# Three rounded products for the second feed-forward product, and a new sharing of the rounding among ScalarE, VectorE and GpSimd

## The chip, the cores and the metric

One Trainium2 chip, one of its cores. The metric is the device time of one execution in microseconds. The kernel before takes 1093.89 us, the median of three runs (1093.78 to 1093.91).

## The reference

Four transformer blocks run one after the other on x of (4, 512, 256) in float32, steered by a conditioning vector of 256 for each of the four sequences. Called layer 0 to layer 3 here:

```
layer 0: h = film(rmsnorm(x)); one head of 256: softmax(q k^T / 16) v; x += out @ wp + b
         h = film(rmsnorm(x)); x += gelu(h @ w1 + b1) @ w2 + b2
layer 1: layernorm, scale and shift; 16 heads of 16, q and k normalised (cosine attention);
         x += gamma1 * (out @ wp + b);  x += gamma2 * (gelu(h @ w1 + b1) @ w2 + b2)
layer 2: layernorm, scale and shift; 16 heads, softmax(q k^T / 4) v; both branches gated as in layer 1
layer 3: 16 heads, softmax(q k^T) / 16; x += out @ wp + b; out = sln(x) + x, no feed-forward part
```

The feed-forward part goes from 256 to 1024 and back to 256, with the exact gelu. Layers 0, 1 and 2 have one.

## The kernel before, in words

Work is cut into 16 jobs, one for each layer and sequence (job j has layer j // 4 and sequence j % 4), each of 512 tokens, that is 4 token tiles of 128 partitions. X stays on the chip, tokens on the partitions.

**One list sets the order.** `PLAN` is a list of steps (kind, job or unit, index), built once from tables of due times (SINGLE0 to SINGLE3, FFN0 to FFN2, QKV, ATTN, FFN, FFN3 and so on, in ticks; a multi-head job has 16 ticks, a job of layer 0 is laid out on the same scale) and of patterns for the pairs of score products (PAIR and its like). Every engine walks through this same list and emits its own part of each step, so the list is the order on every queue: TensorE, ScalarE, VectorE, GpSimd, and SP, which issues all transfers. All waits are on semaphores that count the steps done. In layers 1 to 3 the score products of one job run beside the projections and the feed-forward part of the job before it.

**Precision.** Most products are made of three: an operand is split into a high part, rounded to float32r (`_h`), and a low part, the difference (`_l`), and `product` (L634 to L636) issues high x high, high x low and low x high. A few products use plain float32: the transposes, the weighted sums over V (L751, L790), and the second feed-forward product (L831). A plain float32 matmul appears in the trace as two records.

**A job's feed-forward part.** norm2 gives tok2 (L1155, L1159), TensorE transposes it (hT2, L680), ScalarE scales and shifts it to `postT_f` (L882), VectorE rounds it to `postT_h` (L1059; ScalarE itself in layer 3), and GpSimd subtracts (L1388). fc1 makes 8 banks of 128x512, each by two triples. VectorE adds the bias on the way from the bank to `gT` (L1337). When all is there, the step gelu has ScalarE work in place on `gT`, two tiles of 512 at a time (L996). fc2 multiplies tiles of `gT`, 128 tokens as the stationary operand, with `w2_s` (256 columns moving), 8 products for each of 4 token tiles, one bank each. VectorE adds the bias row (L1344), GpSimd multiplies by the gate where there is one and adds to X (L1421, L1428).

**Layer 0's softmax.** VectorE takes the negated maximum of a bank (L1286) and scales it by 1/16 (L1287). ScalarE exponentiates with that bias and a scale of 1/16 and sums the row (L954). VectorE takes the reciprocal (L1292) and scales the row (L1293). Then the row is transposed (pT0) and multiplied with V. W_v and W_p are merged beforehand, so that this product is already the projection (L790), and VectorE adds it to X (L1312).

**The other layers' softmax.** VectorE reduces a first set of score products (max, L711 on TensorE and L1273 on VectorE), and the shift is folded into the second (scores, L736); ScalarE exponentiates (L944, L941); the weighted sums carry a column of ones for the denominator.

**Banks.** Seven banks of the matmul memory go round as a ring among all kinds of products (`RINGED`); the eighth collects the weighted sums. TensorE claims a bank when the reader of its last content is done.

**Weights.** w_qkv, w_p and w_1 are loaded in pieces of 256 KB. The first eight have places of their own (in `gT` and `probs`), later ones take turns in one buffer, `raw`: SP loads a piece when the one before is split, ScalarE rounds it (L854) and GpSimd subtracts (L1379). w_2 is loaded straight to `w2_s`.

**The rest that the change touches.** q and k: ScalarE writes the rounded part with the bias (L929), VectorE the low part from the same bank (L1243); likewise for the transposed attention output oT2 (L989, L1131). norm1 is on VectorE in layer 0 and on GpSimd (L1408) otherwise; norm2 is on VectorE.

Of the kernel before, what the change touches and what calls it, by code (L numbers as in the profile page):

```python
# [30 lines left out]
SCALE = (DIM ** -0.5, 1.0, HD ** -0.5, 1.0)  # L31
# [33 lines left out]
SINGLE0 = {"stat1": (-35.66,), "norm1": (95.09,), "hT1": (95.15, -51.96), "q": (52.71, 32.6), "k": (44.4, 51.22),  # L65
# [7 lines left out]
SINGLE2 = {"stat1": (-76.02,), "norm1": (-65.07,), "hT1": (-54.95, -50.83), "q": (-42.45, -39.93),
           "k": (-42.44, -37.11), "v": (-46.48, -29.71), "scores0": (-33.39, -32.62, -32.29, -30.97),
           "soft0": (-19.93, -18.73, -8.94, -3.07), "pT0": (-18.64, -15.94, 3.54, 6.39), "proj": (-1.74, 7.24),
           "stat2": (9.09,), "norm2": (11.69,), "bias": (-26.4,)}
FFN0 = {"hT2": (-6.48, -1.66), "fc1": (0.65, 1.43, 2.87, 7.57, 8.57, 10.48, 12.64, 13.3), "gelu": (10.5,),
        "fc2": (17.26, 18.61, 23.07, 32.19)}
FFN2 = {"hT2": (13.21, 13.55), "fc1": (23.3, 23.54, 23.67, 23.99, 25.74, 25.98, 26.03, 27.98), "gelu": (26.69,),
        "fc2": (31.27, 31.92, 33.07, 33.9)}  # L80
FIRST = {("merge", 0, 0): -124.29, ("mergerow", 0, 0): -109.34, ("v", 0, 0): -70.09, ("v", 0, 1): -67.94,
         ("modrow", 0, 1): -98.09, ("headscale", 1, 0): -51.0, ("mod", 0, 1): -57.81, ("split_wp", 0, 0): -182.81,
         ("split_w1", 0, 0): -41.76, ("split_w1", 0, 1): -31.99, ("split_w1", 0, 2): -9.65, ("split_w1", 0, 3): 5.96,
         ("load_w2", 0, 1): -31.88, ("load_w2", 0, 2): -21.35, ("load_w2", 0, 3): -16.6}
NEXT1 = {("modrow", 1, 0): -56.06, ("mod", 1, 0): -41.97, ("load_mod", 1, 1): -52.72, ("modrow", 1, 1): 27.9,
         ("mod", 1, 1): 31.64, ("load_gate", 1, 0): 12.82, ("split_qkv", 1, 0): 26.63, ("load_qkv", 1, 1): 7.49,
         ("split_qkv", 1, 1): 35.43, ("load_qkv", 1, 2): 10.53, ("split_qkv", 1, 2): 46.77,
         ("load_qkv", 1, 0): -34.16, ("vones", 4, 0): 44.63, ("vones", 5, 0): 66.11}
LEAD_IN = {"stat1": (-29.34,), "norm1": (-25.36,), "hT1": (-22.98, -21.7), "qktok": (-18.2, -17.08, -16.9, -16.15),
           "qkss": (-16.92, -16.51, -15.44, -14.66), "qkroot": (-12.97,), "v": (-13.86, -12.83),  # L90
           "qknorm": (-12.92, -12.45, -12.35, -11.47), "q": (-10.22, -9.46), "k": (-9.65, -9.35),
           "stack": (-42.54, -35.32, -7.52, 4.91),
           "gmax": (-8.33, -7.93, -7.8, -6.86, -6.81, -5.35, -5.01, -4.95, -4.89, -4.54, -4.51, -3.48, -3.26, -2.88, -2.52, -2.18),
           "shift1": (-0.73, -0.59), "crow": (-40.19, -34.41, -22.72, 2.06)}
# [5 lines left out]
QKV = {"hT1": (-19.99, -13.91), "q": (-12.79, -9.58), "k": (-11.71, -11.59), "v": (-7.18, -6.37),  # L100
       "stack": (-8.14, -7.62, 1.2, 1.31), "stat1": (-28.09,), "norm1": (-26.73,)}
ATTN = {"oT1": (18.35, 18.35, 18.55, 18.63), "oT2": (19.0, 19.2), "proj": (20.28, 20.87), "stat2": (22.39,),
        "norm2": (24.27,)}
FFN = {"hT2": (25.31, 25.33), "fc1": (27.44, 27.6, 27.96, 28.05, 29.82, 30.13, 30.33, 30.64), "gelu": (30.28,),
# [215 lines left out]
def cond_blocks_kernel(nc, x, cond, cols, rows, wqkv, wp, w1, w2, wmod, wgate, out):  # L320
# [3 lines left out]
    with ExitStack() as ctx:  # L324
# [173 lines left out]
        def by_vector(a):  # L498

            return layer(a) < LAYERS - 1  # L500
# [1045 lines left out]
```

## Time and profile before

| | |
|---|---|
| median of three runs | 1093.89 us |
| the profiled execution | 1094.24 us, its span 1092.5 us |
| TensorE busy | 1062.0 us (97% of the span) |
| VectorE busy | 805.8 us (74%) |
| ScalarE busy | 659.8 us (60%) |
| GpSimd busy | 360.1 us (33%) |
| granted TensorE clock | full in nearly all of the span |

A matmul's record lasts from its start to its modelled end, and the next one starts before that end. So TensorE's busy share says whether it is fed, and the pace of a kind of matmul is read from start to start. In a row of groups stand the line of the kernel, the engine, the operation, what is written and read, the shape, the count, the busy time, the mean of one in ns, and the idle time of the engine just before these instructions with what ended it. The table's lines repeat on the page; the rows further down are those that the argument uses.

### The profile page before, as it was taken

What the parts mean: (1) busy time and instruction counts of PE and PEld (TensorE: products, weight loads), DVE (VectorE), ACT (ScalarE), POOL (GpSimd) and SP (SyncE); (2) the same over time, 40 slices, a digit from 0 to 9 for tenths busy, and PEclk for the clock granted to TensorE, in tenths of its full rate; (3) what the DMA queues carried; (4) which work ended last, traced back from release to release, by engine and by line L of the source; (5) the groups of instructions that cost most, each with busy time, mean ns of one, the idle gap of its engine ahead of it and who ended that gap; (6) DMA issues with size and microseconds to landing.
All of it is one profiled execution on the core that took longest, in us unless ns stands there. A gap on an engine that the chain in (4) does not pass through costs nothing.

```text
span 1092.5 us, 18693 instructions
## 1 busy us (share of the span) xinstructions
PE 1062.0 (97%) x6321; PEld 683.9 (63%) x6321; DVE 805.8 (74%) x1657; ACT 659.8 (60%) x1098; POOL 360.1 (33%) x339
## 2 busy tenths in 40 slices
PE   7999999999999999999999999999999999999995
PEld 5788788755755756657566556566566566645442
DVE  8676658686495584475986986976977967998984
ACT  3453342487467477565675774675765665686764
POOL 3333252422251433611521522422512513441523
PEclk9999999999999999999999999999999999999999
DMA  7100001213313222122122232212202203233301
GB/s 248 59 1 1 10 30 29 60 49 86 89 38 100 73 69 66 37 65 59 43 76 64 55 81 69 60 39 69 67 14 58 59 1 84 59 79 68 89 6 44
DMA packets 36381, 64.39 MB, mean 59 GB/s; under 512 B 7208, under 2 KB 22312, under 8 KB 36288
## 3 DMA queue, kind: packets, MB, share of 16 engines
q1 hardware_dynamic: 36288, 63.20, 21.9%
q8 instruction: 53, 0.87, 0.3%
q14 instruction: 40, 0.33, 0.1%
HBM read 22.90 MB, written 2.12 MB: 23 GB/s over the span
## 4 chain that ended last, share of the span: by engine, by line
PE 84%; DVE 10%; issue 2%; POOL 1%; ACT 1%; DMA 1%; SPq 0%; POOLq 0%; DVEq 0%; ACTq 0%
PE rings L831 15%; PE rings L751 14%; PE rings L736 12%; PE rings L634 10%; PE rings L636 9%; PE rings L635 9%; PE rings L711 4%; PE rings L790 2%; PE rings L680 2%; DVE m L1273 2%; PE rings L795 1%; PE rings L719 1%; PE rings L807 1%; DVE stats L1102 1%; PE rings L661 1%
## 5 line engine op out<-in xcount | busy, mean ns | idle before, releaser
L944 ACT ACTIVATE probs<-rings 128x512 f32<-128x512 f32 x566 | 299.5, 606 | 164.1 <-PE rings L711 96.3
L1273 DVE TENSOR_REDUCE m<-rings 128x1 fp32r<-128x512 f32 x512 | 318.8, 683 | 17.0 <-PE rings L711 14.2
L736 PE MATMUL rings<-SQ,SK 64*128 64x512 f32 x768 | 225.5, 436 | 3.7 <-ACT probs L941 1.1
L736 PEld LDWEIGHTS rings<-SQ,SK 64*128 64x128 f32 x768 | 106.7, 185 | 151.2 <-issue 76.6
L751 PE MATMUL rings<-probs,V 128*32 128x512 f32 x1536 | 198.6, 605 | 1.4 <-issue 1.4
L711 PE MATMUL rings<-SK,SQ 63*128 63x512 f32 x512 | 180.0, 442 | 0.8
L831 PE MATMUL rings<-w_s,gT 128*128 128x256 f32 x768 | 175.3, 382 | 0.3 <-DVE tmp L1344 0.3
L831 PEld LDWEIGHTS rings<-w_s,gT 128*128 128x128 f32 x768 | 142.5, 190 | 25.9 <-DVE gT L1337 3.4
L941 ACT ACTIVATE probs<-rings 128x1024 f32<-128x1024 f32 x101 | 98.2, 1031 | 39.8 <-PE rings L736 20.3
L1337 DVE TENSOR_SCALAR gT<-rings,colv 128x512 f32<-128x512 f32 x96 | 71.1, 748 | 39.7 <-PE rings L636 39.1
L1421 POOL TENSOR_TENSOR tmp<-tmp,gates 128x512 f32<-128x512 f32 x32 | 41.1, 1284 | 169.4 <-DVE tmp L1344 160.1
L711 PEld LDWEIGHTS rings<-SK,SQ 63*128 63x128 f32 x512 | 82.1, 185 | 12.3 <-ACT probs L944 8.9
L1388 POOL TENSOR_TENSOR hT_l<-hT_f,hT_h 128x512 fp32r<-128x512 f32 x30 | 38.7, 1291 | 150.2 <-DVE hT_h L1059 103.5
L1344 DVE TENSOR_TENSOR tmp<-rings,rowp 128x256 f32<-128x256 f32 x48 | 20.3, 424 | 89.3 <-PE rings L831 89.0
L751 PEld LDWEIGHTS rings<-probs,V 128*32 128x32 f32 x1536 | 35.8, 109 | 77.4 <-issue 66.5
L634 PE MATMUL rings<-postT_h,w_h 128*128 128x512 f32 x192 | 79.5, 414 | 0.5 <-POOL postT_l L1388 0.4
L636 PE MATMUL rings<-postT_h,w_l 128*128 128x512 f32 x192 | 75.4, 393 | 0.0
L635 PE MATMUL rings<-postT_l,w_h 128*128 128x512 f32 x192 | 75.3, 392 | 0.0
L1408 POOL TENSOR_SCALAR tok<-X,mv,rstd 128x256 f32<-128x256 f32 x48 | 58.2, 1222 | 39.0 <-PE rings L719 19.9
L1388 POOL TENSOR_TENSOR postT_l<-postT_f,postT_h 128x512 fp32r<-128x512 f32 x24 | 34.7, 1459 | 86.4 <-DVE postT_h L1059 86.4
L1428 POOL TENSOR_TENSOR X<-X,tmp 128x512 f32<-128x512 f32 x40 | 51.4, 1284 | 22.8 <-issue 19.3
L996 ACT ACTIVATE gT<-gT 128x1024 f32<-128x1024 f32 x48 | 47.5, 1048 | 14.9 <-DVE gT L1337 14.6
(196 smaller groups left out, 1808.2 us busy)
## 6 DMA issues: line engine op xcount, KB each, us to landing
SQ<-qh SPq DMA_DIRECT2D x96, 128.0 KB, 2.6
SK<-kh SPq DMA_DIRECT2D x96, 128.0 KB, 2.7
SQ<-ql SPq DMA_DIRECT2D x48, 128.0 KB, 2.7
SK<-kl SPq DMA_DIRECT2D x48, 128.0 KB, 2.9
wmod_s<-in_wmod SPq DMA_DIRECT2D x6, 512.0 KB, 4.4
w_s<-in_w SPq DMA_DIRECT2D x12, 256.0 KB, 3.1
gates<-gate_rows SPq DMA_DIRECT2D x12, 256.0 KB, 3.4
raw<-in_wqkv SPq DMA_DIRECT2D x9, 256.0 KB, 2.9
```

The lines of the kernel that those rows point to most:

```text
L634: pe.matmul(out, sh, mh, start=first, stop=False)
L635: pe.matmul(out, sh, ml, start=False, stop=False)
L636: return pe.matmul(out, sl, mh, start=False, stop=last)
L711: mm = pe.matmul(o[:, :], SQ[a % 4][r:r + KS, n // 2, c * P:(c + 1) * P], SK[a % 4][r:r + KS, n // 2, :], start=True, stop=True)
L736: mm = pe.matmul(o[:, :], SK[a % 4][r:r + KS + 1, n // 2, c * P:(c + 1) * P], SQ[a % 4][r:r + KS + 1, n // 2, :], start=True, stop=True)
L751: mm = pe.matmul(AVB[32 * n:32 * n + 32, :], V[j % 2][:, i, (HD + 1) * h:(HD + 1) * h + 32], probs[:, (4 * t + n) % PROBS, :], start=(i == ...
L831: mm = pe.matmul(o[:, 0:DIM], gT[:, m, i * P:(i + 1) * P], w2_s[:, m, :], start=(m == 0), stop=(m == MT - 1))
L941: act.activation(probs[:, n % PROBS:n % PROBS + 2, :], two_banks(kind, a, i), ACT.Exp, scale=SCALE[layer(unit_job(a))]).then_inc(done["sco ...
L944: act.activation(probs[:, n % PROBS, :], bank(kind, a, i)[:, :], ACT.Exp, scale=SCALE[layer(unit_job(a))]).then_inc(done["scores"], 1)
L1273: nc.vector.tensor_reduce(m16[:, col:col + 1], bank(kind, a, i)[:, :], AX_X, ALU.max, negate=True).then_inc(done["max"], 1)
L1337: nc.vector.tensor_scalar(gT[:, i, :], bank(kind, a, i)[:, :], colv[:, layer(a), C_B1 + i:C_B1 + i + 1], None, ALU.add).then_inc(done[kind ...
L1388: nc.gpsimd.tensor_tensor(lo, full, hi.bitcast(F32), ALU.subtract).then_inc(done[kind], 1)
```

## The change

The second feed-forward product is made of three rounded products. `gT` becomes `gT_f` (full), `gT_h` and `gT_l` with half of the 8 chunks each, so the step is in two halves: gelu, fc2a for chunks 0 to 3, gelu, fc2 for chunks 4 to 7. ScalarE applies gelu straight from the bank with the bias. The rounded part of gelu's result is written by ScalarE in layer 0 (a second gelu), by VectorE in layer 1, by GpSimd in layer 2, and GpSimd makes the low part. w_2 is split like the other weights. One bank now holds two token tiles of the second product. Of hT1 and hT2 the rounded part comes from ScalarE in layer 0, VectorE in layer 1 (as a reduction over an axis of length 1), GpSimd in layers 2 and 3. norm2 is on ScalarE, VectorE, GpSimd, GpSimd in layers 0 to 3. In layer 3 GpSimd makes the low parts of q, k and oT2 from a full copy that ScalarE writes. In layer 0 the scale 1/16 is folded into q's weights and bias, and 1/sum is applied when the projection is added to X. All due times and patterns of the list are new.

```diff
-SCALE = (DIM ** -0.5, 1.0, HD ** -0.5, 1.0)
+SCALE = (1.0, 1.0, HD ** -0.5, 1.0)
+Q_SCALE = DIM ** -0.5
+ROUND_H = ("act", "dve", "pool", "pool")
+ROUND_G = ("act", "dve", "pool")
+NORM1 = "dve"
+NORM2 = ("act", "dve", "pool", "pool")
+POOL_LOW = (False, False, False, True)
...
-FFN = {"hT2": (25.31, 25.33), "fc1": (27.44, 27.6, 27.96, 28.05, 29.82, 30.13, 30.33, 30.64), "gelu": (30.28,),
-       "fc2": (31.96, 33.93, 34.26, 34.85)}
+FFN = {"hT2": (24.03, 24.43), "fc1": (26.28, 26.53, 26.53, 26.91, 29.54, 29.62, 29.68, 29.74), "gelu": (26.46, 29.75),
+       "fc2a": (28.12, 29.23), "fc2": (33.88, 34.54)}
...
-                if kind == "load_w2":
-
-                    if a > 0:
-                        sp.wait_ge(pe_ring, use("fc2", a * BATCH - 1, TT - 1))
-                    sp.dma_start(w2_s[:, 2 * i:2 * i + 2, :], w2[a, DIM * i:DIM * (i + 1), :].rearrange("(c p) n -> p c n", p=P)
-                                 ).then_inc(in_w2[i], 16)
-                elif kind in ("load_qkv", "load_wp", "load_w1"):
+                if kind in ("load_qkv", "load_wp", "load_w1", "load_w2"):
...
-                    pe.wait_ge(done["soft0"], nth("soft0", a, i))
+                    pe.wait_ge(exp0, nth("scores0", a, i))
...
-                elif kind == "fc2":
-
-                    for m in range(MT):
-                        if i == 0:
-                            pe.wait_ge(gated, (nth("gelu", a) - 1) * (MT // 2) + m // 2 + 1)
-                            pe.wait_ge(in_w2[m // 2], 16 * (layer(a) + 1))
-                        mm = pe.matmul(o[:, 0:DIM], gT[:, m, i * P:(i + 1) * P], w2_s[:, m, :], start=(m == 0), stop=(m == MT - 1))
+                elif kind in ("fc2a", "fc2"):
+
+                    h = int(kind == "fc2")
+                    for t in range(2):
+                        tok = (2 * i + t) * P
+                        for m in range(MT // 2):
+                            if i == 0 and t == 0:
+                                pe.wait_ge(g_lo, (nth("gelu", a, h) - 1) * (MT // 2) + m + 1)
+                                pe.wait_ge(done["split_w2"], nth("split_w2", layer(a), 2 * h + m // 2))
+                            mm = product(o[:, t * DIM:(t + 1) * DIM], [x[:, m, tok:tok + P] for x in (gT_h, gT_l)],
+                                         [w[:, h * MT // 2 + m, :] for w in (w2_h, w2_l)], m == 0, m == MT // 2 - 1)
...
+                elif kind == "norm2" and NORM2[layer(a)] == "act":
...
+                    for t in range(TT):
+                        ins = act.activation(tok2[:, t, :], X[:, TT * batch(a) + t, :], ACT.Copy, scale=rstd[:, 1, t:t + 1])
...
                 elif kind == "gelu":
 
-                    for m in range(0, MT, 2):
-                        act.wait_ge(done["fc1"], nth("fc1", a, m + 1))
-                        act.activation(gT[:, m:m + 2, :], gT[:, m:m + 2, :], ACT.Gelu).then_inc(gated, 1)
+                    if i == 0 and READ_BEFORE[(kind, a, i)]:
+                        act.wait_ge(pe_ring, use(*READ_BEFORE[(kind, a, i)]))
+                    if i == 1:
+                        act.wait_ge(pe_ring, use("fc2a", a, 1))
+                    elif a > 0:
+                        act.wait_ge(pe_ring, use("fc2", a - 1, 1))
...
+                    for m in range(i * MT // 2, (i + 1) * MT // 2):
+                        act.wait_ge(pe_ring, use("fc1", a, m))
+                        col = C_B1 + m
+                        for dst in (gT_f, gT_h) if ROUND_G[layer(a)] == "act" else (gT_f,):
+                            ins = act.activation(dst[:, m % (MT // 2), :], bank("fc1", a, m)[:, :], ACT.Gelu,
+                                                 bias=colv[:, layer(a), col:col + 1])
+                        ins.then_inc(done["fc1"], 1)
...
-                    nc.vector.scalar_tensor_tensor(out=hi, in0=full, scalar=1.0, in1=full, op0=ALU.mult, op1=ALU.max
-                                                   ).then_inc(rounded[kind], 1)
+                    nc.vector.tensor_reduce(hi, full.unsqueeze(2), AX_X, ALU.max).then_inc(rounded[kind], 1)
...
+                elif kind == "gelu" and ROUND_G[layer(a)] == "dve":
+                    for m in range(MT // 2):
+                        dve.wait_ge(done["fc1"], nth("fc1", a, i * MT // 2 + m))
+                        nc.vector.tensor_reduce(gT_h[:, m, :], gT_f[:, m, :].unsqueeze(2), AX_X, ALU.max).then_inc(g_hi, 1)
...
-                    link(nc.vector.reciprocal(rc0[:, i:i + 1], sum0[:, i:i + 1]))
-                    nc.vector.tensor_scalar(probs[:, i, :], probs[:, i, :], rc0[:, i:i + 1], None,
-                                            ALU.mult).then_inc(done["soft0"], 1)
+                    nc.vector.reciprocal(rc0[:, a % 2, i:i + 1], sum0[:, i:i + 1]).then_inc(done["soft0"], 1)
...
-                    nc.vector.tensor_scalar(gT[:, i, :], bank(kind, a, i)[:, :], colv[:, layer(a), C_B1 + i:C_B1 + i + 1], None,
-                                            ALU.add).then_inc(done[kind], 1)
...
+                    if ROUND_H[layer(a)] == "pool":
+                        link(nc.gpsimd.tensor_copy(hi, full))
...
+                elif kind == "gelu":
+
+                    for m in range(MT // 2):
+                        if ROUND_G[layer(a)] == "dve":
+                            pool.wait_ge(g_hi, nth_g_hi(a, i, m))
+                        else:
+                            pool.wait_ge(done["fc1"], nth("fc1", a, i * MT // 2 + m))
+                        if ROUND_G[layer(a)] == "pool":
+                            link(nc.gpsimd.tensor_copy(gT_h[:, m, :], gT_f[:, m, :]))
+                        nc.gpsimd.tensor_tensor(gT_l[:, m, :], gT_f[:, m, :], gT_h[:, m, :].bitcast(F32), ALU.subtract
+                                                ).then_inc(g_lo, 1)
```

## Rows read from the trace of the kernel before

**Rows 1.** Four stretches: length, each engine's busy us (instructions), granted clock, DMA share, GB/s.

```profile
0.00:272.00 272.00, 263.48 (x1380) 199.33 (x1381) 192.72 (x435) 127.73 (x197) 88.29 (x86) 1.00 0.19 56
272.00:590.00 318.00, 312.87 (x1903) 198.66 (x1902) 213.08 (x420) 206.45 (x309) 105.60 (x89) 1.00 0.26 67
590.00:914.00 324.00, 323.19 (x1981) 198.85 (x1980) 254.41 (x502) 208.36 (x369) 101.28 (x88) 1.00 0.21 54
914.00:1092.50 178.50, 162.46 (x1064) 87.03 (x1062) 145.62 (x303) 117.23 (x227) 64.96 (x78) 0.98 0.22 57
```

**Rows 2.** Chain that ended last: whole span by engine, then from 1000 us by line.

```profile
PE 84%; DVE 10%; issue 2%; POOL 1%; ACT 1%; DMA 1%; SPq 0%; POOLq 0%; DVEq 0%; ACTq 0%
by line: PE rings L751 21.2%; DVE m L1273 17.2%; PE rings L736 13.6%; PE rings L711 6.7%; issue 6.2%; PE rings L634 3.8%; DVE tok L1304 3.7%; PE rings L636 3.0%; PE rings L635 3.0%; ACT probs L944 1.8%; DVE rcp L1303 1.7%; DVE postT_l L1131
```

**Rows 3.** Second product: groups by line, the chain, and projection triples in order of time.

```profile
L831 PE MATMUL rings<-w_s,gT 128*128 128x256 f32 x768 | 175.3, 382 | 0.3 <-DVE tmp L1344 0.3
...
124.45 3.46 PE rings L831 x16
...
298.71 0.28 PE L634 MATMUL rings<-wp_h,postT_h 128*128 128x256 f32 x1
...
301.42 0.28 PE L636 MATMUL rings<-wp_h,postT_l 128*128 128x256 f32 x1
```

**Rows 4.** Groups by line on VectorE.

```profile
L1273 DVE TENSOR_REDUCE m<-rings 128x1 fp32r<-128x512 f32 x512 | 318.8, 683 | 17.0 <-PE rings L711 14.2 <-PE rings L736 1.1
...
L1337 DVE TENSOR_SCALAR gT<-rings,colv 128x512 f32<-128x512 f32 x96 | 71.1, 748 | 39.7 <-PE rings L636 39.1
...
L1344 DVE TENSOR_TENSOR tmp<-rings,rowp 128x256 f32<-128x256 f32 x48 | 20.3, 424 | 89.3 <-PE rings L831 89.0
L1159 DVE SCALAR_TENSOR_TENSOR tok<-X,mv,rstd 128x256 f32<-128x256 f32 x44 | 19.4, 503 | 4.5 <-POOL rstd L1397 4.5
...
L1243 DVE SCALAR_TENSOR_TENSOR kl<-rings,colv,kh 128x512 fp32r<-128x512 f32 x24 | 17.9, 748 | 5.9 <-ACT kh L929 5.5
...
L1059 DVE SCALAR_TENSOR_TENSOR hT_h<-hT_f 128x512 fp32r<-128x512 f32 x22 | 17.4, 793 | 37.3 <-ACT hT_f L882 37.3
...
L1353 DVE TENSOR_TENSOR tmp<-rings,rowp 128x512 f32<-128x512 f32 x16 | 11.0, 685 | 2.3 <-PE rings L636 1.9
...
L1293 DVE TENSOR_SCALAR probs<-probs,small 128x512 f32<-128x512 f32 x16 | 10.6, 660 | 0.6
...
L1155 DVE SCALAR_TENSOR_TENSOR tok<-X,rstd 128x256 f32<-128x256 f32 x16 | 7.9, 554 | 0.9 <-POOL rstd L1397 0.9
```

**Rows 5.** Groups by line on ScalarE, and a gelu block's end in order of time.

```profile
L996 ACT ACTIVATE gT<-gT 128x1024 f32<-128x1024 f32 x48 | 47.5, 1048 | 14.9 <-DVE gT L1337 14.6
...
L882 ACT ACTIVATE hT_f<-rings,modb,mods 128x512 f32<-128x512 f32 x32 | 24.8, 786 | 17.3 <-PE rings L680 11.4 <-PE rings L636 5.9
...
L929 ACT ACTIVATE qh<-rings,colv 128x512 fp32r<-128x512 f32 x24 | 16.6, 690 | 20.5 <-PE rings L636 20.3
...
L900 ACT ACTIVATE V<-rings 128x256 f32<-128x256 f32 x48 | 15.9, 388 | 9.3 <-PE rings L636 9.2
...
L996 ACT ACT_TABLE_LOAD x12 | 15.4, 1283 | 0.2
...
814.86 1.28 ACT L944 ACT_TABLE_LOAD   x1
816.15 1.09 ACT L944 ACTIVATE probs<-rings 128x512 f32<-128x512 f32 x2
```

**Rows 6.** Groups by line on GpSimd, and GpSimd's longest wait in total.

```profile
L1408 POOL TENSOR_SCALAR tok<-X,mv,rstd 128x256 f32<-128x256 f32 x48 | 58.2, 1222 | 39.0 <-PE rings L719 19.9 <-PE rings L736 19.0
...
L1388 POOL TENSOR_TENSOR hT_l<-hT_f,hT_h 128x512 fp32r<-128x512 f32 x30 | 38.7, 1291 | 150.2 <-DVE hT_h L1059 103.5 <-ACT hT_h L882 46.7
...
L1370 POOL MEMSET SQ<- 128x1024 f32 x4 | 3.8, 952 | 0.2
...
POOL tmp L1421 <- DVE tmp L1344: 160.1, 14, 25.3
```

More of the change, by code:

```diff
@@ L73 @@
[L73 to L78, printed above, removed]
@@ L85 @@
[L85 to L94, printed above, removed]
@@ L100 @@
[L100 to L103, printed above, removed]
-FFN = {"hT2": (25.31, 25.33), "fc1": (27.44, 27.6, 27.96, 28.05, 29.82, 30.13, 30.33, 30.64), "gelu": (30.28,),
-       "fc2": (31.96, 33.93, 34.26, 34.85)}
-FFN3 = {"hT2": (20.5, 21.76), "fc1": (26.98, 27.46, 27.97, 28.8, 29.65, 30.13, 30.38, 30.47), "gelu": (30.81,),
-        "fc2": (33.4, 33.69, 34.29, 34.79)}
@@ L307 @@
         LAST_OF_EIGHTH = _users[RING]
+ORDERED = {kind: [s for s in PLAN if s[0] == kind] for kind in ("hT1", "hT2", "gelu")}
 def nth(kind, a, i=0):
@@ L493, in piece, with by_scalar, nth_rounded, nth_g_hi @@
             if n < len(first_in):
-                where = gT[:, 4 + n, :] if n < 4 else probs[:, n, :]
+                where = gT_f[:, n, :] if n < MT // 2 else probs[:, n, :]
                 return where.rearrange("p (c n) -> p c n", c=CH)
             return raw[:, :, :]
+        def by_scalar(a):
+            return NORM1 == "act" and 0 < a < BATCH
         def by_vector(a):
-            return layer(a) < LAYERS - 1
+            return ROUND_H[layer(a)] == "dve"
+        def nth_rounded(kind, a, i):
+            return sum(ROUND_H[layer(b)] == "dve" for _, b, _ in ORDERED[kind][:nth(kind, a, i)])
+        def nth_g_hi(a, i, m):
+            return MT // 2 * sum(ROUND_G[layer(b)] == "dve" for _, b, _ in ORDERED["gelu"][:nth("gelu", a, i) - 1]) + m + 1
         block = ctx.enter_context(nc.Block())
@@ L880, in _ @@
                     full = postT_f if second else hT_f
-                    for dst in (full[:, i, :],) if by_vector(a) else (full[:, i, :], hi[:, i, :]):
+                    for dst in (full[:, i, :], hi[:, i, :]) if ROUND_H[layer(a)] == "act" and (kind, a, i) not in EARLY else (full[:, i, :],):
                         ins = act.activation(dst, bank(kind, a, i)[:, :], ACT.Identity,
@@ L1120, in _ @@
                                             ALU.add).then_inc(done[kind], 1)
-                elif kind == "oT2":
+                elif kind == "oT2" and (a == JOBS - 1 or not POOL_LOW[layer(a)]):
                     dve.wait_ge(hi_in[kind], nth(kind, a, i))
@@ L1143, in _ @@
                     ins.then_inc(done[kind], 1)
-                elif kind == "norm2":
+                elif kind == "norm2" and NORM2[layer(a)] == "dve":
                     l, b = layer(a), batch(a)
@@ L1221, in _ @@
                                                    ).then_inc(done[kind], 1)
-                elif kind in ("q", "k"):
+                elif kind in ("q", "k") and not POOL_LOW[layer(a)]:
                     l = layer(a)
@@ L1306, in _ @@
                                             ).then_inc(done[kind], 1)
+                elif kind == "proj" and layer(a) == 0:
+                    dve.wait_ge(pe_ring, use(kind, a, i))
+                    dve.wait_ge(done["bias"], nth("bias", a))
+                    for t in (2 * i, 2 * i + 1):
+                        x = X[:, TT * batch(a) + t, :]
+                        dve.wait_ge(done["soft0"], nth("soft0", a, t))
+                        ins = nc.vector.scalar_tensor_tensor(out=x, in0=bank(kind, a, i)[:, DIM * (t % 2):DIM * (t % 2 + 1)],
+                                                             scalar=rc0[:, a % 2, t:t + 1], in1=x, op0=ALU.mult, op1=ALU.add)
+                    ins.then_inc(done[kind], 1)
                 elif kind == "proj" and direct(a) and a < JOBS - 1:
```

264 lines of the change are left out of this document (161 added, 103 removed), and 19 rows, old and new, of tables (FIRST, SINGLE0, SINGLE1, SINGLE2).

## The prediction

> **What bounds the kernel now.** I read the busy time by stage first, then the chain of waits, then the groups by line of TensorE, VectorE, ScalarE and GpSimd, and last the order of time around one feed-forward product and one table switch. The four stretches [rows 1] are layer 0 (to 272 us), layer 1 (to 590), layer 2 (to 914) and layer 3 with the tail. In layers 0 to 2 TensorE is busy 263 of 272, 313 of 318 and 323 of 324 us at the full clock; nobody else passes 79% of a stretch (VectorE in layer 2, 254 of 324). The chain that ended last says the same: TensorE 84%, VectorE 10%, the others 1 or 2% each [rows 2]. VectorE matters mainly at the end, where the maxima of the scores (m, L1273) alone are 17% of the chain's last 92.5 us. So a microsecond taken from TensorE's stream in layers 0 to 2 should come off the span; one taken from VectorE counts at about a tenth; one added to ScalarE or GpSimd counts only where it makes TensorE wait.
>
> **TensorE: the second feed-forward product.** Its 384 full-precision products (12 jobs, 4 token tiles, 8 chunks; each appears as two matmul records, 768 in all) are TensorE's largest removable block. Sixteen records stand 3.46 us in the chain [rows 3], 0.216 us a record, 0.432 us a product; 384 of these are 166 us, the chain's 15% of L831. After the change each is three rounded matmuls of the same shape, 128x128 stationary and 256 columns moving. The same shape in the same triple is in the trace already, in the attention projection: from its first to its last record are 23 steps in 301.42 - 298.71 = 2.71 us [rows 3], 0.118 us each with the weight loads of 190 ns hidden. A product becomes 0.353 us, all 384 become 136 us. **Gain 30.2 us**, 2.5 us per job. Nothing else is added to TensorE: scores, transposes and the other products keep number and size. That the trace has this very triple excludes for me that the change doesn't do what it says on this engine.
>
> **VectorE.** It loses the 96 biased copies of the first product, 71.1 us; the scaling of probs in layer 0, 10.6 (the 16 short scalings of the maxima go too, not counted); the rounding of hT in layers 0 and 2, 30 instructions of 0.74 (L1059: 17.4 us for 22, taken for both tiles) = 22.4 (each remaining one 0.683 as a reduction, like L1273: another 1); the low parts of q, k, oT2 in layer 3, 22 x 0.748 = 16.4; norm2 of layer 0, 7.9, and 28 of 44 instructions of norm2 in layers 2 and 3, 12.3 [rows 4]. It gains 32 reductions that round gelu's result in layer 1, 32 x 0.683 = 21.9; the sums of the second product, 48 evictions of 128x512 at 0.685 = 32.9 instead of 20.3; and about 1 us where the projection of layer 0 is scaled tile by tile. Net: 71.1 + 10.6 + 22.4 + 1.0 + 16.4 + 20.2 - 21.9 - 12.6 - 1.3 = **106 us less of 806** (the four stretches of rows 1 together), 13%. If its 10% of the chain (109 us) shrinks in that proportion, 14 us come off. Bounds: 0, if the places where it ends a wait are untouched; 28, if backlog falls twice as fast as work. I take 14, since it loses work in layers 0, 2 and 3 (10 us per job in layer 2, by the same rows) and none in layer 1.
>
> **ScalarE.** Gelu now reads the bank and adds the bias: 96 x 0.69 (L929, bank to 128x512 with a bias) = 66.2 instead of 47.5; layer 0 repeats each for the rounded copy, 22.1; the repeated hT of layer 0, 14 x 0.79 = 11.0; norm2 of layer 0, 16 x 0.39 = 6.2 (by L900, 128x256); second copies of q, k, oT2 in layer 3, 22 x 0.69 = 15.2, less the second hT1 there, 6.3; 12 pieces of w2, at most 12 x 0.69 = 8.3 [rows 5]. Gelu comes in two steps per job, with exponentials of the next window between them in nearly every job, so 12 more loads of gelu's table and 12 more of exp's, 24 x 1.283 = 30.8. Sum **+106 of 660**, 70% of the span: no bound by itself. What is queued behind a gelu block on ScalarE are the exponentials; TensorE's weighted sums over V wait for these, and cover is the seven score banks and the other products. A block was 1.28 + 4 x 1.05 + 1.28 = 6.8 us, once a job; it becomes 1.28 + 4 x 0.69 + 1.28 = 5.3 us, twice. In the order of time the load at 814.86 follows the last gelu within 0.02 us and the next exponential stands at 816.15: a switch costs 1.28 us and nothing behind it [rows 5].
>
> The Trainium skill (ScalarE: Activation LUTs, What ACT_TABLE_LOAD costs) gives 1283 ns for the load, which the trace has, and another 1380 ns of drain, which the trace doesn't show; by the page the 24 loads would cost 64 us of ScalarE instead of 31. Its rule to batch calls by set speaks against splitting gelu; the rival below prices what splitting does here, from rows.
>
> **GpSimd.** It gains the low parts of gelu's result, 96 x 1.29 = 123.8, of w2, 12 x 1.29 = 15.5, of q, k and oT2 in layer 3, 22 x 1.29 = 28.4; norm2 in layers 2 and 3, 28 x 1.222 = 34.2; and 56 rounding copies of 128x512 (24 of hT in layers 2 and 3, 32 of gelu in layer 2) that the trace doesn't show [rows 6]. Bounds for one: 0.48, half of the 128x1024 fill, and 1.29, the two-input form; I take 0.9, 50 us in all (27 to 72). Sum **+252, 360 to 612 us**, 56% of the span. It is now on a path: gelu's part m waits for ScalarE, (copy and) subtraction, then the second product, and TensorE's whole queue stands behind that wait. For half a job in layer 2 this is 4 x (0.9 + 1.29) = 8.8 us from first to last, in layers 0 and 1 5.2. Cover is what stands between gelu and fc2a in the new tables: 1.7 ticks in layers 1 and 2, about 8 us at 16 ticks to a window of 81 us (324 / 4), with two more ticks where the tiles overlap. Behind a late gelu on GpSimd stand the gate multiplications, which before spent 160 us waiting for VectorE [rows 6], so there is room.
>
> ScalarE and GpSimd have about 1% of the chain each, 11 us. In proportion to their added work (16% and 70%) that is 2 + 8 = **10 us back**. Bounds: 0, all hidden, and the rivals below.
>
> **The rest.** Pieces of w2 now take turns in the one raw buffer: 12 more loads on SP that wait for the split before them (some 3 us of transfer, 0.6 of ScalarE, 1.3 of GpSimd); behind them on SP stand the stack transfers, which are issued 6 ticks, some 30 us, ahead. Cost 0; with that cover gone, up to 5 us for each of the eight after layer 0, 40 us. The scaling of q's weights at the start is folded into instructions that are there. pT0 waits for the exponential instead of the scaled rows: a shorter path in layer 0, but with TensorE at 97% there I count nothing. The order of all steps is new; it can give or take, with the same rows as bound (what is not TensorE in the chain, 16% or 175 us), and I take 0.
>
> **Sum**, against the profiled execution's own 1094.24 us (span 1092.5, some 1.7 around it; the median of the runs is 1093.89, so nothing to convert): 1094.2 - 30.2 - 14 + 10 = **1060 us**.
>
> **Rivals.**
> *VectorE was the partner in the bursts.* Three maxima of 0.683 against bursts of score pairs: if its backlog, not TensorE's own rate, sets the pace in layer 2 and the tail, its relief gives the upper bound of 28 and the added work hides: 1094.2 - 30.2 - 28 = 1036. For it: 79% busy in layer 2, 82% after 914 us. Against: TensorE shows next to no idle time in layer 2.
> *GpSimd is late in layer 2.* If its copies cost the two-input price, half a job takes 4 x 2.58 = 10.3 us, 2.3 beyond the cover of 8; if that stands bare in each of the 8 halves, it adds 18 us: 1078. For it: the copy is the one price the trace doesn't show, and part m waits for two instructions in a row. Against: in the new tables the later half has over three ticks before its sum. It decides over the copy's price, from about 1.1 us each.
> *Gelu in two blocks holds the exponentials (slower).* The mechanism is TensorE standing at the weighted sums while ScalarE switches, works and switches back, 24 times instead of 12. If the added 12 blocks are bare, 12 x 5.3 = 64 us: 1094.2 - 30.2 + 64 = 1128. It decides from 30.2 / 12 = 2.5 us of bare time per added block. For it: blocks longer than any single wait that seven banks cover at one score in 0.6 us (4.2 us). Against: before, blocks of 6.8 us are there and ScalarE has 1% of the chain.
>
> **How the numbers follow.** Forecast 50%, by itself 1048 to 1072; VectorE's relief 20%; GpSimd late 19%; gelu's blocks 11%, from 1090 upwards. The range is 1034 to 1082: it holds the first three but for the outer part of each, and leaves out the fourth. This kernel's measurement tells apart about 0.2%, 2.2 us. Faster 0.88, within 0.2% 0.02, slower 0.10, nearly all of it from the blocks.
>
> **What would show it.** The second product as 1152 records at 0.118 us, TensorE's time in it near 136 us; VectorE near 698 us, ScalarE near 766 with 48 table loads, GpSimd near 612; in the windows of layers 1 and 2 some 78 us per job instead of 80; 1152 records spread wider than 0.118, or TensorE idle ahead of them behind g_lo, would speak for GpSimd; idle ahead of the V sums behind exponentials, next to table loads, for the blocks. The forecast is wrong if TensorE's busy share falls under 94%, or if windows of layer 2 lose more than 5 us each.

## The result, and the profile after

The changed kernel takes 1074.77 us (median of three runs, 1074.04 to 1075.45) against 1093.89: ratio 0.9825, 95% interval 0.9803 to 0.9848. Run again in five rounds it gave 1073.64 us and 0.9810 (0.9796 to 0.9823). The second, narrower ratio is the base of all differences below, in microseconds of a kernel of 1094.4. The gain is 20.8 us where 34 were forecast: the sign and the range of 1034 to 1082 held, the size was off by 13, and the time lies outside the 1048 to 1072 that the forecast gave itself without its rivals.

The first profiled execution took 1075.45 us, its span 1073.7. Busy time and the chain that ended last:

```profile
PE 1042.4 (97%) x6705; PEld 681.8 (64%) x6705; DVE 693.3 (65%) x1474; ACT 743.9 (69%) x1253; POOL 584.9 (54%) x553
...
PE 56%; POOL 4%; DVE 4%; issue 3%; DMA 1%; SPq 1%; ACT 1%; POOLq 0%; DVEq 0%; ACTq 0%
```

Forecast were VectorE near 698, ScalarE near 766, GpSimd near 612. TensorE is as busy as before, in a shorter span. Its idle time is the same, too: 1092.5 - 1062.0 = 30.5 us before, 1073.7 - 1042.4 = 31.3 now. The shares of the chain can't be compared with [rows 2] as they stand: they add up to 70%, since this chain can be followed back only to 327.7 us. From there to the end VectorE has 38 us of it and GpSimd 46; before, from 327.6 us on, they had 60 and 7. What this is worth is read below.

Four stretches, cut where the layers' feed-forward parts end (they answer to [rows 1]):

```profile
0.00:268.00 268.00, 255.94 (x1459) 198.92 (x1460) 137.28 (x346) 166.26 (x273) 125.03 (x117) 0.99 0.18 53
268.00:582.00 314.00, 310.35 (x2086) 199.55 (x2085) 208.48 (x427) 229.32 (x348) 155.86 (x134) 1.00 0.27 70
582.00:902.00 320.00, 318.79 (x2140) 204.40 (x2139) 219.02 (x437) 226.38 (x399) 207.42 (x201) 1.00 0.23 57
902.00:1073.00 171.00, 157.28 (x1025) 78.97 (x1023) 128.57 (x265) 121.95 (x234) 96.56 (x104) 0.97 0.22 59
```

TensorE stands idle 12 us in layer 0 and 14 in the tail (before 9 and 16), and 5 between. From the end of one job's second product to that of the next, layer 1 takes 75.6 us per job (588.2 - 285.9, over 4; before 77.4) and layer 2 78.6 (before 80.9). By the end of layer 0 the kernel is 3.5 us ahead where four jobs at 2.5 should have made it 10; layer 1 adds 7.3, layer 2 9.2, and the rest takes back 1.3. The second product alone should have given 30 us, and the span is 18.8 shorter. Of the 11 us between, 6.5 are lost in layer 0: there job 0 ends 6.7 us ahead, jobs 1 and 2 take 1.0 and 3.0 us longer than before, and job 3 gains 0.8.

The second product, the groups that answer to L831 in [rows 3]:

```profile
L666 PE MATMUL rings<-w_h,gT_h 128*128 128x256 f32 x384 | 109.9, 286 | 0.0
...
L667 PE MATMUL rings<-w_l,gT_h 128*128 128x256 f32 x384 | 106.8, 278 | 0.0
L668 PE MATMUL rings<-w_h,gT_l 128*128 128x256 f32 x384 | 106.7, 278 | 0.0
```

1152 records as foreseen; in order of time they stand 0.118 us apart (24 of them from 205.3 to 208.1, where only the first step is longer, 0.23). The last column is what TensorE waited for ahead of them: nothing. GpSimd, which makes the low parts, was never late for them.

VectorE, ScalarE and GpSimd, groups by line (they answer to [rows 4, 5, 6]):

```profile
L1352 DVE TENSOR_REDUCE m<-rings 128x1 fp32r<-128x512 f32 x512 | 319.5, 681 | 76.8 <-PE rings L743 55.5 <-PE rings L768 20.4
...
L1425 DVE TENSOR_TENSOR tmp<-rings,rowp 128x512 f32<-128x512 f32 x40 | 27.6, 691 | 53.6 <-PE rings L668 51.7 <-DMA rowp<-in_rows 1.4
L1333 DVE TENSOR_REDUCE gT_h<-gT_f 128x512 fp32r<-128x512 f32 x32 | 20.7, 680 | 20.2 <-ACT gT_f L1065 19.7
```

```profile
L1065 ACT ACTIVATE gT_f<-rings,colv 128x512 f32<-128x512 f32 x96 | 64.1, 689 | 24.1 <-PE rings L668 22.1
...
L1065 ACT ACT_TABLE_LOAD x22 | 28.2, 1283 | 45.1 <-PE rings L668 44.9
...
L1065 ACT ACTIVATE gT_h<-rings,colv 128x512 fp32r<-128x512 f32 x32 | 22.2, 695 | 0.0
```

```profile
L1471 POOL TENSOR_TENSOR gT_l<-gT_f,gT_h 128x512 fp32r<-128x512 f32 x96 | 121.8, 1288 | 61.5 <-DVE gT_h L1333 30.7 <-ACT gT_h L1065 28.2
...
L1501 POOL TENSOR_SCALAR tok<-X,mv,rstd 128x256 f32<-128x256 f32 x28 | 33.9, 1223 | 0.2
...
L1470 POOL CAST gT_h<-gT_f 128x512 fp32r<-128x512 f32 x32 | 19.5, 610 | 23.1 <-ACT gT_f L1065 23.1
```

The maxima take the same 319 us, but VectorE now waits 76.8 us for them instead of 17.0: it has the slack that the forecast gave it, and uses it for waiting. The one price that the trace of before did not show, GpSimd's copy, is 0.61 us, within its bounds and under the 0.9 taken. Gelu's step has 22 loads, with 22 that lead back to exponentials: 44, not 48, since two pairs of blocks have no exponential between them. Ahead of these loads ScalarE is idle for 45.1 us in all, most of it until TensorE has filled fc1's bank; before, 14.9 us stood ahead of gelu [rows 5].

### The profile page after: what moved, and what is told of

It is laid out like the page before. It is cut to its first block, busy times and chain, and to the rows that moved or that the text cites. A ratio compares the mean times of both kernels' runs of the same rounds, so it can differ in the third digit from the quotient of the medians.

```text
span 1073.7 us, 19671 instructions
## 1 busy us (share of the span) xinstructions
PE 1042.4 (97%) x6705; PEld 681.8 (64%) x6705; DVE 693.3 (65%) x1474; ACT 743.9 (69%) x1253; POOL 584.9 (54%) x553
## 4 chain that ended last, share of the span: by engine, by line
PE 56%; POOL 4%; DVE 4%; issue 3%; DMA 1%; SPq 1%; ACT 1%; POOLq 0%; DVEq 0%; ACTq 0%
PE rings L783 12%; PE rings L768 10%; PE rings L666 9%; PE rings L668 8%; PE rings L667 8%; PE rings L743 4%; DVE m L1352 2%; PE rings L712 1%; PE rings L827 1%; PE rings L839 1%; POOL tok L1501 1%; SPq L614 1%; DMA raw<-in_w 1%; POOL tmp L1525 0%; DVE tok L1379 0%
## 5 line engine op out<-in xcount | busy, mean ns | idle before, releaser
L1352 DVE TENSOR_REDUCE m<-rings 128x1 fp32r<-128x512 f32 x512 | 319.5, 681 | 76.8 <-PE rings L743 55.5
L768 PE MATMUL rings<-SQ,SK 64*128 64x512 f32 x768 | 229.5, 438 | 5.1 <-ACT probs L998 3.3
L768 PEld LDWEIGHTS rings<-SQ,SK 64*128 64x128 f32 x768 | 107.0, 185 | 147.4 <-issue 67.7
L743 PE MATMUL rings<-SK,SQ 63*128 63x512 f32 x512 | 182.0, 445 | 0.7 <-ACT probs L1001 0.5
L1471 POOL TENSOR_TENSOR gT_l<-gT_f,gT_h 128x512 fp32r<-128x512 f32 x96 | 121.8, 1288 | 61.5 <-DVE gT_h L1333 30.7
L666 PE MATMUL rings<-w_h,gT_h 128*128 128x256 f32 x384 | 109.9, 286 | 0.0
L667 PE MATMUL rings<-w_l,gT_h 128*128 128x256 f32 x384 | 106.8, 278 | 0.0
L668 PE MATMUL rings<-w_h,gT_l 128*128 128x256 f32 x384 | 106.7, 278 | 0.0
L743 PEld LDWEIGHTS rings<-SK,SQ 63*128 63x128 f32 x512 | 81.7, 185 | 15.6 <-ACT probs L1001 12.4
L1065 ACT ACTIVATE gT_f<-rings,colv 128x512 f32<-128x512 f32 x96 | 64.1, 689 | 24.1 <-PE rings L668 22.1
L666 PEld LDWEIGHTS rings<-w_h,gT_h 128*128 128x128 f32 x384 | 72.3, 188 | 3.7 <-DVE m L1352 2.1
L667 PEld LDWEIGHTS rings<-w_l,gT_h 128*128 128x128 f32 x384 | 72.3, 188 | 0.2
L668 PEld LDWEIGHTS rings<-w_h,gT_l 128*128 128x128 f32 x384 | 72.3, 188 | 0.0
L1461 POOL TENSOR_TENSOR postT_l<-postT_f,postT_h 128x512 fp32r<-128x512 f32 x24 | 31.7, 1326 | 56.8 <-DVE postT_h L1131 29.5
```

The lines of the kernel that those rows point to most:

```text
L666: pe.matmul(out, sh, mh, start=first, stop=False)
L667: pe.matmul(out, sh, ml, start=False, stop=False)
L668: return pe.matmul(out, sl, mh, start=False, stop=last)
L743: mm = pe.matmul(o[:, :], SQ[a % 4][r:r + KS, n // 2, c * P:(c + 1) * P], SK[a % 4][r:r + KS, n // 2, :], start=True, stop=True)
L768: mm = pe.matmul(o[:, :], SK[a % 4][r:r + KS + 1, n // 2, c * P:(c + 1) * P], SQ[a % 4][r:r + KS + 1, n // 2, :], start=True, stop=True)
L1065: ins = act.activation(dst[:, m % (MT // 2), :], bank("fc1", a, m)[:, :], ACT.Gelu, bias=colv[:, layer(a), col:col + 1])
```

## The experiments

"Over the changed kernel" means over 0.9810. The order of the list is kept unless the diff shows otherwise. The diffs are written short: `...` stands for indices and arguments that stay as they are.

**The products put back.** Each triple becomes one plain float32 product of the rounded parts; everything else stays.

```diff
-mm = product(o[...], [... for x in (gT_h, gT_l)], [... for w in (w2_h, w2_l)], ...)
+mm = pe.matmul(o[...], gT_h[...].bitcast(F32), w2_h[...].bitcast(F32), ...)
```

> The changed kernel with the second feed-forward product as plain float32 matmuls of the rounded parts, one of 2 records in place of three rounded ones (the low parts are left out of the product; all other work, the order and the waits stay). If TensorE's stream sets the time wherever this product stands, the 30 us that the three products saved come back: 1074.8 + 30 = 1105 us, more than before. If the new order and the sharing of the rounding are themselves the gain, most of it stays: under 1090.

Measured 1107.31 us, ratio 1.0117 (1.0102 to 1.0132): 33.6 us over the changed kernel, where the working had 30.2. The ratio says more: with the products as before, all the rest of the change costs 12.8 us over the kernel before (the ratio's 0.0117). The forecast had this rest at -14 + 10 = -4.

**Two of three products.** The product w_l x gT_h is left out.

```diff
-mm = product(...)
+pe.matmul(out, gT_h[...], w2_h[...], start=(m == 0), stop=False)
+mm = pe.matmul(out, gT_l[...], w2_h[...], start=False, stop=(m == MT // 2 - 1))
```

> The changed kernel with two rounded products in place of three in the second feed-forward product (high x low of the weights is left out): 384 matmuls fewer at 0.118 us, 45 us less for TensorE, nothing else changed. If TensorE's stream alone sets the time, 1074.8 - 45 = 1030; if the gain fades because ScalarE and VectorE become the pace of the windows, a half of it: 1045 to 1055.

Measured 1041.0 us, 0.9511 (0.9489 to 0.9532): 32.7 us less for 384 x 0.118 = 45.3 us of TensorE, 0.72 per microsecond. So most of what is taken from TensorE's stream here comes off the time, and not all of it.

**Half of each maximum**, in both kernels: each reduction reads 256 of its 512 columns. These maxima start at 472 us in the kernel before, so the runs say nothing of VectorE in layer 0 and in most of layer 1.

```diff
-nc.vector.tensor_reduce(m16[...], bank(kind, a, i)[:, :], AX_X, ALU.max, ...)
+nc.vector.tensor_reduce(m16[...], bank(kind, a, i)[:, 0:256], AX_X, ALU.max, ...)
```

> The kernel before with each of the 512 maxima (L1273) taken over 256 of its 512 columns (the other half is left out of the maximum): about 0.27 us less each, some 136 us less on VectorE, in its own order. If VectorE's relief counts by its share of the chain of waits (0.13 us per us), 1094 - 18 = 1076; if by what putting work back cost in the changed kernel (27 us for 68), up to 40 or 50 us less; if TensorE's order sets the time and VectorE is never late in the old order, 1090 to 1094.

> The changed kernel with the same halved maxima, some 136 us less on VectorE. If its new order has used up the relief (it is laid out so that VectorE is just in time, and more relief brings little), 1070 to 1075; if VectorE still holds TensorE, 1060 or less.

The group of maxima, first in the kernel before with that edit, then in the changed one:

```profile
L1273 DVE TENSOR_REDUCE m<-rings 128x1 fp32r<-128x256 f32 x512 | 188.2, 417 | 96.2 <-PE rings L711 88.5 <-PE rings L736 4.8
```

```profile
L1352 DVE TENSOR_REDUCE m<-rings 128x1 fp32r<-128x256 f32 x512 | 189.9, 417 | 160.3 <-PE rings L743 139.7 <-PE rings L768 17.2
```

Before: 1088.2 us, 0.9942 (0.9927 to 0.9957), 6.3 us for 131 us of VectorE, 0.05 per microsecond. Changed: 1068.37 us, 0.9761 (0.9747 to 0.9776), 5.4 us for 128, 0.04. The relief turns into idle time, here as well. At this rate the 106 us that the change takes off VectorE would be worth 5 us and not 14; that is an estimate, since some 55 of them lie in layer 0 (192.7 us busy in its stretch before, 137.3 now).

**Gelu's tables left out**, in both kernels: a function that needs no table of its own stands for gelu, so that no switch is left (ScalarE has 44 instructions fewer in the changed kernel and 24 fewer in the one before, which are the loads).

```diff
-ins = act.activation(dst[...], bank("fc1", a, m)[:, :], ACT.Gelu, ...)
+ins = act.activation(dst[...], bank("fc1", a, m)[:, :], ACT.Identity, ...)
```

```diff
-act.activation(gT[:, m:m + 2, :], gT[:, m:m + 2, :], ACT.Gelu)
+act.activation(gT[:, m:m + 2, :], gT[:, m:m + 2, :], ACT.Copy)
```

> The changed kernel with a biased copy in place of gelu (gelu is left out, so ScalarE needs no other function table; instructions and waits stay). If gelu's two blocks per job hold the exponentials back, the 44 table loads of 1.28 us (56 us of ScalarE, 7 of them or so stay) are what ate the missing 11 to 15 us: 1060 to 1065. If TensorE's stream sets the time and ScalarE has cover, within 3 us of the changed kernel: 1072 to 1076.

> The kernel before with a copy in place of gelu (gelu left out), so that its 12 blocks need no table switches. In the changed kernel this brought 6 us. If the cost is by block, half of it here, 2 to 4 us: 1090 to 1092; if the old order hid its single, longer block, nothing: 1093.5 to 1094.5; if it hid it worse, 6 us or more.

Changed: 1068.66 us, 0.9762 (0.9746 to 0.9777), 5.3 us less. Before: 1094.31 us, 0.9994 (0.9984 to 1.0003), nothing. So the single block was hidden and the two are not wholly: they cost some 5 us, about 0.45 a job. The 45 us of idle time ahead of the table loads are where this can come from: the exponentials queued behind gelu wait with it. This last step is argued; the runs show the price alone. The mechanism of the rival on the slower side exists at a twelfth of its price of 5.3 us a block.

**The sharing put back on VectorE** in layers 2 and 3, then in layer 2 alone and in layer 3 alone.

```diff
-ROUND_H = ("act", "dve", "pool", "pool")
-ROUND_G = ("act", "dve", "pool")
-NORM2 = ("act", "dve", "pool", "pool")
-POOL_LOW = (False, False, False, True)
+ROUND_H = ("act", "dve", "dve", "dve")
+ROUND_G = ("act", "dve", "dve")
+NORM2 = ("act", "dve", "dve", "dve")
+POOL_LOW = (False, False, False, False)
```

> The changed kernel with VectorE again making the rounded parts of hT in layers 2 and 3 and of gelu in layer 2, norm2 in layers 2 and 3, and the low parts of q, k and oT2 in layer 3 (some 68 us more on VectorE, 96 us less on GpSimd). If VectorE's relief is worth nothing because TensorE's stream sets the time, within 4 us: 1071 to 1079. If it is worth what the chain of waits suggested (a tenth), 7 us or more slower, 1082 and up; if GpSimd's added work was what cost time, faster, under 1070.

> The changed kernel with VectorE again making, in layer 2 alone, the rounded parts of hT and gelu and norm2: some 40 us more on VectorE. Taking 131 us from VectorE brought only 6 or 7 us in either kernel, so if what counts is VectorE's mean load, 2 us: 1077; if an order laid out for one sharing breaks under another, a third to a half of the 27 us that all the parts together cost: 1084 to 1088.

> The changed kernel with VectorE again making, in layer 3 alone, the low parts of q, k and oT2, the rounded part of hT1 and norm2: some 27 us more on VectorE. By mean load 1 to 2 us: 1076; if the order breaks, the rest of the 27 us: 1088 to 1092. The two together tell whether the parts add up.

| put back | VectorE, us | time, us | ratio (95%) | over the changed kernel |
|---|---|---|---|---|
| layers 2 and 3 | +66 | 1102.43 | 1.0071 (1.0052 to 1.0091) | +28.6 |
| layer 2 | +42 | 1085.41 | 0.9911 (0.9894 to 0.9927) | +11.1 |
| layer 3 | +28 | 1095.35 | 1.0005 (0.9990 to 1.0019) | +21.3 |

The parts add up to 32.4, within what the intervals leave. They cost 0.27 and 0.76 us per microsecond, five to fifteen times what the halved maxima gave. The longest waits of TensorE with layer 3 put back:

```profile
PE rings L768 <- DVE ql L1318: 4.5, 2, 2.3
PE rings L768 <- DVE m L1352: 4.5, 1, 4.5
```

In the changed kernel the second is 0.3 us, and in place of the first stands 0.2 us for kl. The list was laid out with these steps on GpSimd; with the same list they arrive in front of VectorE's maxima, and the score products wait. These two waits are 9.0 of the 21.3 us; the granted clock is lower as well, 0.94 over the 188 us after 902 where the changed kernel has 0.97. So I don't read these runs as a price of VectorE's time, but as a sign that the new order and the new sharing belong together; a list laid out anew for the old sharing was not run.

**Two places of the new order.** In the changed kernel the first product of q starts at 17.84 us, before it was 14.64. TensorE's first work there, and the stretch from 8 to 16 us (the kernel before, the changed one):

```profile
8.65 1.88 PE L661 MATMUL rings<-wmod_s,condT 128*4 128x512 f32 x4 [1.75 <-issue]
...
8.00:16.00 8.00, 5.88 (x26) 3.13 (x27) 6.39 (x20) 2.04 (x3) 1.27 (x2) 1.00 1.09 354
```

```profile
10.58 3.16 PE L693 MATMUL rings<-wmod_s,condT 128*4 128x512 f32 x4 [3.12 <-issue]
...
8.00:16.00 8.00, 4.68 (x18) 1.80 (x19) 2.38 (x12) 0.92 (x2) 1.28 (x2) 0.79 0.94 313
```

The load of the modulation weights is issued behind one more piece of w_qkv, at 3.26 us instead of 2.75; the four products start 1.9 us later and then also run at a lower granted clock (0.79 over the stretch). The second place is at 169 us, where hT2 of job 2 comes close ahead of fc1 and TensorE waits 2.16 us for GpSimd's low part. The edit moves one load forward and one back, and puts v of job 4 into the gap:

```diff
-START = [stat1, load_w1 0, norm1, load_qkv 0, modrow, mod, load_mod 0, load_qkv 2, split_qkv 0, load_mod 1, hT1 0, load_qkv 1, load_w1 2, load_wp, ...]
+START = [stat1, load_w1 0, load_mod 0, norm1, load_qkv 0, modrow, mod, load_qkv 2, split_qkv 0, hT1 0, load_qkv 1, load_w1 2, load_wp, load_mod 1, ...]
+_v = ("v", 4, 0)
+PLAN.remove(_v)
+PLAN.insert(PLAN.index(("fc1", 2, 0)), _v)
```

> The changed kernel with two edits of the order alone: at the start the load for the first modulation goes ahead of the first piece of w_qkv (as before the change) and the second modulation's load behind that of w_p; and the v product of job 4 stands ahead of the first fc1 of job 2, where TensorE stood idle for 2.2 us and then ran at half clock for 3.4 us. My theory, losses in single places of the new order: first q product at about 15 us instead of 17.8, and 2 to 3 us less at the second place: 1069 to 1071 in all. Rival, that each such gain is given back at the next wait: 1074 to 1076.

> The changed kernel itself, in five rounds, as the common base of the differences of a few microseconds (the two orders, gelu's blocks, the maxima over half of the columns). If its first ratio, 0.9825, holds to 0.001, the repaired order is worth 3 to 4 us (its ratio is 0.9793) and leaving gelu's tables out 6 to 7 us (0.9762). If the first comparison was 0.002 too high, the ratio comes near 0.9805: the repaired order is then worth 1 to 2 us and not to be told from nothing, and gelu's blocks 4 to 5 us.

Measured 1071.61 us, 0.9793 (0.9774 to 0.9811): the fastest version that leaves nothing out, 1.9 us under the changed kernel, though the two intervals overlap. The traces are plainer: job 0's second product ends at 118.1 us instead of 122.1, the span is 1068.6 instead of 1071.6 (the second profile of the changed kernel). What is won at the start is kept to the end: 3.0 us by these two traces, 1.9 by the medians (the profiled execution is 1.2 us under its own). The second place brought nothing: of the 2.16 us for GpSimd 0.8 are left, and instead TensorE waits 2.1 us, once, for VectorE's part of layer 1's q and k. The same stretch in this kernel:

```profile
8.00:16.00 8.00, 5.90 (x26) 3.23 (x27) 5.86 (x21) 2.04 (x3) 1.28 (x2) 1.00 1.08 366
```

**The repaired order with layer 0's rounding of gelu and norm2 on VectorE.** The same order edit, and:

```diff
-ROUND_G = ("act", "dve", "pool")
-NORM2 = ("act", "dve", "pool", "pool")
+ROUND_G = ("dve", "dve", "pool")
+NORM2 = ("dve", "dve", "pool", "pool")
```

> The changed kernel with the two edits of the order (start, v of job 4) and with VectorE in ScalarE's place for the rounded part of gelu and for norm2 in layer 0 (32 second gelus of 0.69 us and 16 short instructions leave ScalarE). If ScalarE's second pass delays layer 0, 2 to 4 us better than the order's edits alone: 1068 to 1070; if TensorE is fed there anyway, the same 1071 to 1072; if the order breaks, 1074 and more.

Measured 1080.95 us, 0.9873 (0.9856 to 0.9889): 8.8 us over the repaired order, with 23 us less on ScalarE. Now the second product does wait:

```profile
L670 PE MATMUL rings<-w_h,gT_h 128*128 128x256 f32 x384 | 111.2, 290 | 3.3 <-POOL gT_l L1475 2.3 <-issue 0.9
```

With this list, ScalarE's second gelu in layer 0 is dear in busy time and cheap where it stands. The wait in the second product is 3.3 of the 8.8 us. The whole loss falls into layer 0: job 1's second product ends at the same time as in the repaired order (155.1 and 155.5 us), job 2's 8.0 us later (217.6 and 209.6). Here, too, the list was not laid out anew.

## Why the prediction was right, and where not

**The second product: right.** 1152 records at 0.118 us as read from the projection's triple, no wait ahead of them. Put back, the products cost 33.6 us where the working had 30.2; one of the three left out returns 0.72 us per microsecond. From the start of each record to the start of the next on TensorE, the second product took 169.7 us before and takes 136.9 now. This one term is why the sign held. That the range held is in part luck: it was stretched to 1082 for a late GpSimd, which did not come.

**VectorE: the term that was mis-sized.** Busy time was forecast well (698, measured 693). The step from busy time to span failed: "If its 10% of the chain (109 us) shrinks in that proportion, 14 us come off." A share of the chain is no price. Of TensorE's idle time, the waits that VectorE ends are only 11.3 us before, against the chain's 109, and 7.3 in the changed kernel (summed from the list of waits); and both runs with halved maxima gave 0.04 to 0.05 us per microsecond, which makes 5 us for 106 by the estimate above. That is 9 of the 13 us. The tail says the same: after job 11's second product it takes 169.9 us before (922.6 to 1092.5) and 171.2 and 169.7 in the two profiles of the changed kernel, with 13 us less on VectorE. The rival that gave VectorE 28 falls with it.

**ScalarE: right in kind, and now with a price.** "2 + 8 = 10 us back" for ScalarE and GpSimd together had 2 for ScalarE; gelu in two blocks costs 5. ScalarE's busy time rose by 84 us and not by 106, but the sum was of durations of instructions, and these rose by 103 (748.1 to 850.7): neighbouring records overlap (850.7 us of durations stand in 743.9 us of busy time), and busy time counts the overlap once. Each load took 1283 ns, as read. For the 8 us that GpSimd had in this term no run gives a price; what the trace shows is one wait of 2.2 us, for the low part at 169 us.

**GpSimd late in the second product: wrong.** The copy costs 0.61 us, half a job in layer 2 takes 4 x (0.61 + 1.29) = 7.6 us, within the cover of 8, and the wait is 0.0. The chain goes through GpSimd elsewhere, in layer 3, which the forecast didn't name; but it is not where time is lost. First the chain, then two lines of the list of waits:

```profile
916.73 4.78 POOL tok L1501 x4
922.80 2.48 POOL kl L1508 x2
929.09 3.02 DMA SK<-kl
...
1031.01 4.83 POOL tok L1501 x4
...
1053.65 11.28 issue
```

```profile
PE rings L743 <- DMA SK<-kl: 0.2, 1, 0.2
...
POOL tmp L1560 <- DVE X L1405: 11.7, 2, 11.4
```

norm2 of a job takes 4.8 us there; on VectorE it took 4 x 0.50 = 2.0 [rows 4]. But behind the first of these stretches TensorE is idle only 0.2 us for the key, and behind the second GpSimd itself is idle for 11.4 us, until VectorE's X is there (the chain's 11.28 us of "issue"). A quicker GpSimd would have lengthened that idle time. The same holds as for VectorE: GpSimd has 33 us of the chain after 902 us, and hardly a wait of TensorE. That is read from the trace; no run tests it.

**The new order: taken as 0, it was not.** Its start loses 2 to 3 us, which the repaired order gets back.

**The sum.** Beside the products the change costs 12.8 us. Runs give a price for gelu's blocks, 5.3, and for the start, 1.9 (3.0 by the traces); VectorE's relief gives 5 back by the estimate. That leaves 9.5 to 10.6 us that no run prices, and 3.4 fewer if the products are worth only their own 30.2.

The traces say where on TensorE the time stands. It is not in the idle time, which is nearly the same. So I take for each record the time from its start to the start of the next one on TensorE, and sum it by kind of product (the last record to the end of the span; the changed kernel by its second profile):

| us | before | changed | repaired order |
|---|---|---|---|
| second product | 169.7 | 136.3 | 136.9 |
| other products by triples | 357.0 | 352.6 | 353.3 |
| 1280 score products (L711 and L736, now L743 and L768) | 227.2 | 233.6 | 233.9 |
| transposes and others with the unit matrix | 81.9 | 86.1 | 86.2 |
| weighted sums over V | 189.5 | 191.2 | 191.2 |
| the rest | 65.2 | 69.7 | 65.2 |

The start's loss is in the last row. The largest other loss is in the score products, 6.4 us. VectorE's maxima don't hold them: with these halved in both kernels the difference is 8.7 us (221.3 and 230.0). Gelu's tables explain a part: left out in both, the difference is 3.9 (227.0 and 230.9). Two score products can start together:

```profile
1008.76 0.39 PE L768 MATMUL rings<-SQ,SK 64*128 64x512 f32 x1
1008.77 0.39 PE L743 MATMUL rings<-SK,SQ 63*128 63x512 f32 x1
```

Before, 570 of the 1280 start less than 0.03 us ahead of the next record, and 569 and 570 in the two experiments on that kernel; with the new patterns of pairs 530 to 544. So what is left of this loss may come from the patterns, which the change also made new. That is argued, as no run puts the old ones back, and it is some 4 of the 10 us; the transposes' 4 us, and jobs 1 and 2 in layer 0, stay open.

## What to carry to other kernels

Price relief on an engine that is not the bound by the waits it ends, or halve its largest group and look: its share of the chain of waits made it nearly three times too dear here. The list of TensorE's waits in the trace of before already held the smaller number. Where one list sets the order of all engines, a list and the sharing of work that it was laid out for are one change: trying the sharing alone on the list measures the misfit. Compare the first 20 us of both traces first; a load issued one place later cost 2 to 3 us here, and nothing later won them back. And where an engine is busy 97% of the time before and after, its busy share says nothing: sum the time from start to start by kind of instruction.

## What the runs showed of the hardware

**The same idle time and two clocks.** At 169 us TensorE waits 2.16 us in both profiled executions of the changed kernel. First execution, then second, in order of time:

```profile
171.66 0.79 PE L666 MATMUL rings<-postT_h,w_h 128*128 128x512 f32 x1 [2.16 <-POOL postT_l L1461]
172.25 0.63 PE L667 MATMUL rings<-postT_l,w_h 128*128 128x512 f32 x1
172.68 0.63 PE L668 MATMUL rings<-postT_h,w_l 128*128 128x512 f32 x1
```

```profile
172.54 0.50 PE L666 MATMUL rings<-postT_h,w_h 128*128 128x512 f32 x1 [2.16 <-POOL postT_l L1461]
172.87 0.39 PE L667 MATMUL rings<-postT_l,w_h 128*128 128x512 f32 x1
173.10 0.40 PE L668 MATMUL rings<-postT_h,w_l 128*128 128x512 f32 x1
```

In the first the products follow 0.43 us apart until 174.8, at a granted clock of 0.50, which is the level of 1.2 GHz; in the second 0.23 us apart at a granted clock of 1.00, 2.4 GHz. An idle stretch of this length may or may not take the clock down: one profile can show 1 to 2 us that the next one doesn't.

**VectorE held up by GpSimd.** In the first execution GpSimd's subtraction of 128x512 runs from 170.34 to 171.60. VectorE, in order of time:

```profile
169.46 0.29 DVE L1285 SCALAR_TENSOR_TENSOR rs<-tok,rs 128x128 f32<-128x128 f32 x1
...
170.44 1.31 DVE L1285 SCALAR_TENSOR_TENSOR rs<-tok,rs 128x128 f32<-128x128 f32 x1
```

The same instruction takes 0.29 us and, started inside GpSimd's, 1.31: it ends 0.15 us after GpSimd's does. The Trainium skill (SBUF — State Buffer, Who interferes with whom) says that VectorE and GpSimd share a port pair under an exclusive lock; this row agrees. As a mean over its 12 instructions L1285 takes 466 ns where L1281 and L1283 of the same shape take 292. More work on GpSimd can thus cost VectorE something that no group of GpSimd's shows. It does not touch every instruction: the 512 maxima, which read a bank, take 681 ns in the mean with GpSimd busy 585 us, and 683 before with 360.
